# A selective-scan layer with a grouped expert layer: the scan's matmuls 64 rows wide, and LayerNorm and softplus work moved in two instruction queues

## The chip, the cores and the metric

The kernel runs on one core of one Trainium2 chip. A core has TensorE (PE in the profile, its weight loads PEld), VectorE (DVE), ScalarE (ACT), GpSimd (POOL) and SyncE (SP), which here issues the DMA transfers. Each engine works through its own list of instructions in order, and semaphores tie the lists together. The metric is the device time of one execution in microseconds.

## The reference

The input x is 16 sequences of 1024 tokens with 512 channels. It is normalised once (xn), and two branches are added to it. The second branch (routing tokens to experts) lies in the later phases of the kernel, which the change does not touch. The first is a chunked selective scan:

```python
def _forward(x, W_in, dt_W, dt_b, A_log, D_param, W_out, norm_w):
    proj = x @ W_in.T            # xp, z, B_ssm, C_ssm, dt_low
    dt = jax.nn.softplus(dt_low @ dt_W.T + dt_b)
    dA = dtc * A
    dAcs = jnp.cumsum(dA, axis=2)
    ...
    scores = jnp.einsum('bcihn,bcjhn->bcijh', Cc, Bc) * Lm * dtc[:, :, None, :, :]
    y_intra = jnp.einsum('bcijh,bcjhp->bcihp', scores, xc)
    ...
    y_cross = jnp.einsum('bcthn,bchnp,bcth->bcthp', Cc, h_states, jnp.exp(dAcs))
    y = (y_intra + y_cross).reshape(B, S, H, P)
    y = y + xp * D_param[None, None, :, None]
    y = y.reshape(B, S, D_INNER)
    rms = jnp.sqrt(jnp.mean(y * y, axis=-1, keepdims=True) + 1e-06)
    y = y / rms * norm_w
    y = y * jax.nn.silu(z)
    return y @ W_out.T
...
x = x + _L0_attn_ref(xn, ...) + _L0_ffn_ref(xn, ...)
```

There are 16 heads of 32 channels, 16 states per head, and chunks of 64 tokens.

## The kernel before

The kernel has three phases: the scan layer (to about 2170 us), the gather and the scatter of the expert layer (the rest). All three parts of the change lie in the first phase.

The first phase handles 128 tiles of 128 tokens (two chunks each), two tiles to a superstep, so 64 supersteps `s` and two more to drain. In superstep s every engine works on three generations at once: tiles 2s and 2s+1 (n0: projections, step sizes), tiles 2(s-1) and 2(s-1)+1 (n1: scores, states, scan), and tiles 2(s-2) and 2(s-2)+1 (n2: gate, output projection, residual). The order of the work is written out by hand for each engine, in a loop over s.

- TensorE, per superstep: `project_bdt`, `transpose_xn`, `transpose_b`, `project_x`, `transpose_yz`, `chunk_states`, `scores`, `project_z`, `project_out`, `sums`, `scan`, and then much the same for the second tile of each pair. `transpose_yz(n2)` writes the bank `mix` that `lo_xn` reads, so it waits for `lo_xn`. `scores` waits for `expand_c`. `sums(s)` waits for `dA_ready`, the last of POOL's `step_sizes`, and stands right ahead of `scan(n1)`. `scan(n)` waits for `mask_scores(n)`. Each fp32 matmul of `scan`, `scores` and `chunk_states` is recorded as two instructions.
- VectorE: `scale_y`, `lo_xn`, `expand_c`, `gate`, `stats`, `finish_stats`, `normalize`, `lo_yz`, `states`, `mask_scores`, `residual`, `states`, `scale_y`, and the same for the second tile; `picks(s)` ends the superstep. `stats(n)` waits for the DMA that brings tile n of x; `normalize` for POOL's `inv_std`; `lo_yz` for ScalarE's `hi_yz`.
- SyncE issues the load of x tile 2(s+2) only after it has issued the store of `residual(n2)`, and the load of tile 2(s+2)+1 only after `picks(s)` and the store of `residual(n2+1)`. The DVE reads tile 2(s+2) in superstep s, and tile 2(s+2)+1 in superstep s+1.
- ScalarE: after the bias is added by POOL (`add_bias`) it takes Abs, Relu and Exp of it, then `hi_yz(n2)`, `copy_x`, Ln and Exp (which need POOL's `exp_low`), `spread_c`.
- GpSimd: `add_skip`, `add_bias`, `inv_std`, `exp_low`, `spread_c`, `step_sizes`, `skip_x`, `inv_rms`, `scale_b`, `add_skip`, `inv_std`, `spread_c`, `skip_x`, `inv_rms`.

Of the kernel before, what the change touches and what calls it, by code (L numbers as in the profile page):

```python
# [32 lines left out]
H, HD, NS, R = 16, 32, 16, 16  # L33
DI = H * HD
KI = DI // P
CH = 64
# [55 lines left out]
def attention_phase(nc, io, keep, sems):  # L92
# [5 lines left out]
    with ExitStack() as ctx:  # L98
        scan_bank = ctx.enter_context(nc.psum_tensor("a_scan", [P, 4, 512], F32))
# [4 lines left out]
    HALF = 256  # L104
# [6 lines left out]
    scan_in = [sb(f"scan_in{c}", [P, H, CH]) for c in range(2)]  # L111
# [50 lines left out]
    xs = [[sb(f"xs{c}_{j}", [P, H, HD]) for j in range(4)] for c in range(2)]  # L162
# [109 lines left out]
    def valid(s):  # L272
        return 0 <= s < NST

    def token_rows(c):
        return slice(CH * c, CH * c + CH)
# [16 lines left out]
    def states_ready(n, c):  # L293

        return 4 + 8 * n + 4 * c
# [48 lines left out]
    def gpsimd_program(pool, gather):  # L344
# [23 lines left out]
        def skip_x(n):  # L368

            pool.wait_ge(x_cp, n + 1)  # L370
            wait(pool, yv_cp, n)
            for c in range(2):
                rows_ = token_rows(c)
                nc.gpsimd.tensor_tensor(dx[rows_, :], xs[c][n % 4][rows_, :, :].rearrange("t h d -> t (h d)"), d_row[rows_, :],  # L374
                                        ALU.mult).then_inc(dx_cp, 1)
                pool.wait_ge(dx_cp, 2 * n + c + 1)
# [65 lines left out]
        for s in range(NST + 2):  # L442
            n1, n2 = 2 * (s - 1), 2 * (s - 2)
            add_bias, exp_low, step_sizes = soft_plus(s)
            if valid(s - 2):
                add_skip(n2 + 1)
            if valid(s):
                add_bias()
            if valid(s + 1):
                inv_std(2 * (s + 1) + 1, 1)  # L450
            if valid(s):
                exp_low()
            if valid(s - 1):
                spread_c(n1)
            if valid(s):
                step_sizes()
            if valid(s - 1):
                skip_x(n1)
            if valid(s - 2):
                inv_rms(n2 + 1, 1)  # L460
            if valid(s):
                scale_b(s)
            if valid(s - 1):
                add_skip(n1)
            if valid(s + 2):
                inv_std(2 * (s + 2), 0)
            if valid(s - 1):
                spread_c(n1 + 1)
                skip_x(n1 + 1)
                inv_rms(n1, 0)  # L470
# [147 lines left out]
    def vector_program(dve):  # L618
# [14 lines left out]
        def stats(n):  # L633
            dve.wait_ge(x_in[n % (2 * STB)], 16 * (n // (2 * STB) + 1))
            wait(dve, xn_ready, n - 1)
            nc.vector.bn_stats(bst[:, n % 2, :], x_tile(n)).then_inc(ln, 1)
            dve.wait_ge(ln, 2 * n + 1)

        def finish_stats(n):
            nc.vector.bn_aggr(mv[:, n % 2, :], bst[:, n % 2, :]).then_inc(ln, 1)  # L640
# [8 lines left out]
        def lo_xn(n, b, i):  # L649
            dve.wait_ge(xnT_hi, n + 1)  # L650
            nc.vector.tensor_tensor(xnT[b][1][:, :, i * P:(i + 1) * P], mix[:].rearrange("p (k t) -> p k t", k=KD),
                                    xnT[b][0][:, :, i * P:(i + 1) * P].bitcast(F32), ALU.subtract).then_inc(xnT_lo, 1)
# [41 lines left out]
        def scale_y(n):  # L694

            dve.wait_ge(y_ps, 2 * n + 2)
            wait(dve, yv_cp, n)
            gain = e1[:, n // 2 % 2, n % 2, :].rearrange("p (b h) -> p b h", b=2).unsqueeze(3).to_broadcast([P, 2, H // 2, HD])
            nc.vector.tensor_tensor(yt[:].rearrange("p (b h d) -> p b h d", b=2, h=H // 2),  # L699
                                    scan_bank[:, 2:4, HALF:512].rearrange("p b (h d) -> p b h d", h=H // 2), gain,  # L700
                                    ALU.mult).then_inc(yt_cp, 1)
# [51 lines left out]
        for s in range(NST + 2):  # L753
            n0, n1, n2 = 2 * s, 2 * (s - 1), 2 * (s - 2)
            par = s % 2
            gains, next_gains = mg[:, 1 - par, :, :], mg[:, par, :, :]
            if valid(s - 2):
                scale_y(n2 + 1)
            if valid(s + 1):
                lo_xn(2 * (s + 1), 1 - par, 0)  # L760
            if valid(s - 1):
                expand_c(n1)
            if valid(s - 2):
                gate(n2 + 1)
            if valid(s + 1):
                stats(2 * (s + 1) + 1)
                finish_stats(2 * (s + 1) + 1)
                normalize(2 * (s + 1) + 1)
            if valid(s - 2):
                lo_yz(n2)  # L770
            if valid(s - 1):
                dve.wait_ge(mg_ready, s)
                states(n1, 0, gains[:, :, 1:2], gains[:, :, 2:3])
                mask_scores(n1)
            if valid(s - 2):
                residual(n2, 0)
            if valid(s - 1):
                states(n1, 1, gains[:, :, 3:4], gains[:, :, 4:5])

                scale_y(n1)  # L780
            if valid(s + 1):
                lo_xn(2 * (s + 1) + 1, 1 - par, 1)
            if valid(s - 1):
                expand_c(n1 + 1)
                gate(n1)
            if valid(s + 2):
                stats(2 * (s + 2))
                finish_stats(2 * (s + 2))
            if valid(s - 2):
                lo_yz(n2 + 1)  # L790
            if valid(s - 1):
                states(n1 + 1, 0, gains[:, :, 5:6], gains[:, :, 6:7])
                mask_scores(n1 + 1)
            if valid(s + 2):
                normalize(2 * (s + 2))
            if valid(s - 2):
                residual(n2 + 1, 1)
            if valid(s - 1):
                if valid(s):
                    dve.wait_ge(mg_ready, s + 1)  # L800
                    states(n1 + 1, 1, gains[:, :, 7:8], None if s % STB == 0 else next_gains[:, :, 0:1])
            if s == 0:
                stage_lo(LAST_STAGE)
            if valid(s):
                picks(s)

    def tensor_program(pe, gather):
# [113 lines left out]
        def scan(n):  # L921

            pe.wait_ge(mt_cp, 4 * n + 4)
            pe.wait_ge(cs_cp[0], n + 1)
            pe.wait_ge(cs_cp[1], 2 * n + 2)
            pe.wait_ge(g_ready, states_ready(n, 1))
            for h in range(H):
                for c in range(2):
                    for i in range(0, CH, 32):
                        out = scan_bank[CH * c + i:CH * c + i + 32, 2 + h // 8, HALF + h % 8 * HD:HALF + (h % 8 + 1) * HD]  # L930
                        last = nc.tensor.matmul(out, scan_in[c][:, h, i:i + 32], xs[c][n % 4][:, h, :], start=True, stop=True)  # L931
                    if h == H - 1:
                        last.then_inc(y_ps, 1)

# [662 lines left out]
```

## Time and profile before

| | |
|---|---|
| time, median of 3 runs | 3144.28 us (3142.84 to 3148.3) |
| the profiled execution's own time | 3142.84 us |
| its span | 3140.9 us |
| PE busy | 2957.3 us, 94% |
| PEld busy | 2523.2 us, 80% |
| DVE busy | 2407.3 us, 77% |
| ACT busy | 1587.4 us, 51% |
| POOL busy | 1283.6 us, 41% |
| share of PE in the chain that ended last | 82% |
| share of DVE in it | 10% |

The span runs from the first to the last instruction of the program. The chain that ended last is followed back from the last instruction to whatever released each step. The busy time of PE is modelled for pipelined matmuls, so how long a stretch of matmuls takes is read from the start of one group to the start of the next.

### The profile page before, as it was taken

What the parts mean: (1) busy time and instruction counts of PE and PEld (TensorE: products, weight loads), DVE (VectorE), ACT (ScalarE), POOL (GpSimd) and SP (SyncE); (2) the same over time, 40 slices, a digit from 0 to 9 for tenths busy, and PEclk for the clock granted to TensorE, in tenths of its full rate; (3) what the DMA queues carried; (4) which work ended last, traced back from release to release, by engine and by line L of the source; (5) the groups of instructions that cost most, each with busy time, mean ns of one, the idle gap of its engine ahead of it and who ended that gap; (6) DMA issues with size and microseconds to landing.
All of it is one profiled execution on the core that took longest, in us unless ns stands there. A gap on an engine that the chain in (4) does not pass through costs nothing.

```text
span 3140.9 us, 134679 instructions
## 1 busy us (share of the span) xinstructions
PE 2957.3 (94%) x59784; PEld 2523.2 (80%) x59784; DVE 2407.3 (77%) x3546; ACT 1587.4 (51%) x3614; POOL 1283.6 (41%) x2029
## 2 busy tenths in 40 slices
PE   7999999999999999999999999997878877999999
PEld 6888888888888888888888888885766666888887
DVE  5888888888888988898888888885444436777775
ACT  4555555555555555555555555553333322555555
POOL 3555565655555655556555555553000001000000
PEclk9999999999999999999999999998999997999999
DMA  3221111111111111111111111114444435768765
GB/s 113 71 61 48 55 51 51 55 48 55 54 44 55 54 47 55 51 50 53 51 55 51 48 57 52 47 43 173 134 118 119 109 110 154 228 211 236 223 206 156
DMA packets 336546, 286.94 MB, mean 91 GB/s; under 512 B 52304, under 2 KB 265808, under 8 KB 335072
## 3 DMA queue, kind: packets, MB, share of 16 engines
q1 hardware_dynamic: 335392, 278.16, 29.8%
q8 instruction: 473, 7.75, 1.0%
q14 instruction: 105, 0.86, 0.1%
q10 hardware_dynamic: 576, 0.17, 0.0%
HBM read 165.01 MB, written 113.25 MB: 89 GB/s over the span
## 4 chain that ended last, share of the span: by engine, by line
PE 82%; DVE 10%; issue 5%; DMA 1%; POOL 1%; SPq 0%; ACT 0%; DVEq 0%; POOLq 0%; ACTq 0%
PE a_proj L811 34%; PE a_mix L811 9%; PE s_rt L1462 8%; PE g_pick_ps L1223 5%; PE a_scan L931 5%; PE s_w_ps L1448 5%; PE s_sum L1475 4%; DVE g_picked L1192 3%; PE g_acc_ps L1244 2%; DVE scan_in L673 2%; PE a_scan L908 2%; DVE xs L691 2%; PE a_scan L895 2%; PE a_mix L819 2%; PE a_mix L883 2%
## 5 line engine op out<-in xcount | busy, mean ns | idle before, releaser
L691 DVE TENSOR_SCALAR xs<-gs,mg 64x128 f32<-64x128 f32 x960 | 546.7, 628 | 8.8
L811 PE MATMUL a_proj<-wdh,xnTh 128*128 128x512 f32 x1024 | 424.3, 414 | 1.4 <-DVE wdl L627 0.7
L1418 DVE TENSOR_TENSOR s_resT<-s_w_ps,s_b 128x2048 f32<-128x2048 f32 x128 | 293.4, 2292 | 154.3 <-PE s_w_ps L1448 154.3
L1412 ACT COPY s_res<-s_rt 128x512 f32<-128x512 f32 x512 | 263.0, 600 | 290.0 <-PE s_rt L1462 290.0
L811 PE MATMUL a_proj<-wdh,xnTl 128*128 128x512 f32 x1024 | 405.9, 396 | 0.7 <-issue 0.7
L811 PE MATMUL a_proj<-wdl,xnTh 128*128 128x512 f32 x1024 | 404.7, 395 | 0.6 <-issue 0.6
L673 DVE COPY_PREDICATED scan_in<-mask,a_scan 64x512 f32<-64x512 uint32 x512 | 377.5, 737 | 16.0
L382 POOL TENSOR_TENSOR yv<-yt,dx 128x512 f32<-128x512 f32 x128 | 166.6, 1302 | 418.3 <-DVE yt L699 418.3
L374 POOL TENSOR_TENSOR dx<-xs,d_row 64x512 f32<-64x512 f32 x256 | 329.3, 1286 | 15.1
L1192 DVE COPY g_picked<-g_pick_ps 128x1024 f32<-128x1024 f32 x128 | 156.7, 1224 | 224.9 <-PE g_pick_ps L1223 224.9
L540 ACT ACTIVATE scan_in<-CT,hsel 64x128 f32<-64x128 f32 x1024 | 325.9, 388 | 4.8
L365 POOL TENSOR_TENSOR scan_in<-CT,hsel 64x512 f32<-64x512 f32 x256 | 267.1, 1044 | 10.2
L505 ACT COPY raw<-a_proj 128x272 f32<-128x272 f32 x128 | 49.5, 387 | 419.3 <-PE a_proj L811 419.3
L1170 ACT COPY g_picked<-g_pick_ps 128x1024 f32<-128x1024 f32 x128 | 129.6, 1013 | 249.9 <-PE g_pick_ps L1223 249.3
L1462 PE MATMUL s_rt<-s_ident,s_resT 128*128 128x128 f32 x2048 | 255.2, 278 | 0.0
L1462 PEld LDWEIGHTS s_rt<-s_ident,s_resT 128*128 128x128 f32 x2048 | 219.7, 141 | 30.6 <-issue 25.4
L811 PEld LDWEIGHTS a_proj<-wdh,xnTh 128*128 128x128 f32 x1024 | 195.0, 190 | 46.6 <-issue 11.5
L811 PEld LDWEIGHTS a_proj<-wdh,xnTl 128*128 128x128 f32 x1024 | 194.8, 190 | 45.0 <-issue 1.3
L811 PEld LDWEIGHTS a_proj<-wdl,xnTh 128*128 128x128 f32 x1024 | 195.3, 191 | 34.5 <-issue 1.5
L811 PE MATMUL a_proj<-xnTh,wth 128*128 128x256 f32 x768 | 222.0, 289 | 0.0
L811 PE MATMUL a_mix<-woh,ygh 128*128 128x512 f32 x512 | 210.9, 412 | 8.9 <-DVE ygl L711 8.9
L811 PE MATMUL a_proj<-xnTh,wtl 128*128 128x256 f32 x768 | 215.8, 281 | 0.0
(121 smaller groups left out, 6839.3 us busy)
## 6 DMA issues: line engine op xcount, KB each, us to landing
x<-in_x_dram SPq DMA_DIRECT2D x128, 256.0 KB, 3.4
xn_dram<-xn SPq DMA_DIRECT2D x128, 256.0 KB, 2.4
part_dram<-res SPq DMA_DIRECT2D x128, 256.0 KB, 2.9
g_xn<-xn_dram SPq DMA_DIRECT2D x128, 256.0 KB, 3.0
s_w<-in_w_dram SPq DMA_DIRECT2D x128, 256.0 KB, 3.9
s_part<-part_dram SPq DMA_DIRECT2D x128, 256.0 KB, 3.7
out_dram<-s_out SPq DMA_DIRECT2D x128, 256.0 KB, 2.8
g_w<-in_w_dram SPq DMA_DIRECT2D x4, 2048.0 KB, 12.8
```

The lines of the kernel that those rows point to most:

```text
L365: nc.gpsimd.tensor_tensor(c_places(1, w), src, sel, ALU.mult).then_inc(cs_cp[1], 1)
L374: nc.gpsimd.tensor_tensor(dx[rows_, :], xs[c][n % 4][rows_, :, :].rearrange("t h d -> t (h d)"), d_row[rows_, :], ALU.mult).then_inc(dx_cp, 1)
L382: nc.gpsimd.tensor_tensor(yv[:], yt[:], dx[:], ALU.add).then_inc(yv_cp, 1)
L540: last = nc.scalar.activation(dst[:, :, j, :], CT[own, n % 4, :, 0:CH], ACT.Copy, scale=hsel4[own, j:j + 1])
L673: nc.vector.copy_predicated(dst, mask[rows_, :].unsqueeze(1).unsqueeze(1).to_broadcast([CH, 4, 2, CH]), src).then_inc(mt_cp, 1)
L691: nc.vector.tensor_scalar(dst, gs[rows_, q, :].unsqueeze(1).to_broadcast([CH, 2, 2 * HD]), scale0[rows_, q, :], scale1[rows_, q, :], ALU.m ...
L811: last = nc.tensor.matmul(out, lhs[a], rhs[c], start=(k == 0 and n == 0), stop=(k == nk - 1 and n == 2))
L931: last = nc.tensor.matmul(out, scan_in[c][:, h, i:i + 32], xs[c][n % 4][:, h, :], start=True, stop=True)
L1192: nc.vector.tensor_copy(picked_view(n, tq, 1), pick_view(1)).then_inc(pick_cp[1], 1)
L1412: nc.scalar.copy(res[:, n % 4, :, :], rt_bank[n % 3][:].rearrange("p (n d) -> p n d", n=GPT)).then_inc(res_cp, 1)
L1418: nc.vector.tensor_tensor(resT[m % 2][:, :, sets].rearrange("p n (q r) -> p n q r", r=4), w2_bank[:].rearrange("p r q n -> p n q r"), b2[: ...
L1462: last = nc.tensor.transpose(rt_bank[n % 3][:, g * P:(g + 1) * P], resT[m % 2][:, place_of(GPT * t + g), :], ident[:])
```

## The change

It has three parts. On TensorE, `scan(n)` computes each head and chunk in one matmul with 64 output rows, where it took two with 32 rows each. On VectorE, `stats` of either tile of a pair moves ahead of `lo_xn`, `expand_c` and `gate`, with `lo_xn` between `stats` and `finish_stats`; `normalize` of the odd tile stays behind `gate`. On GpSimd, `add_bias` moves behind `inv_std`, `spread_c` ahead of `exp_low`, and `skip_x` ahead of `step_sizes`.

```diff
@@ gpsimd_program @@
             if valid(s - 2):
                 add_skip(n2 + 1)
-            if valid(s):
-                add_bias()
             if valid(s + 1):
                 inv_std(2 * (s + 1) + 1, 1)
             if valid(s):
+                add_bias()
+            if valid(s - 1):
+                spread_c(n1)
+            if valid(s):
                 exp_low()
             if valid(s - 1):
-                spread_c(n1)
+                skip_x(n1)
             if valid(s):
                 step_sizes()
-            if valid(s - 1):
-                skip_x(n1)
@@ vector_program @@
             if valid(s + 1):
+                stats(2 * (s + 1) + 1)
                 lo_xn(2 * (s + 1), 1 - par, 0)
+                finish_stats(2 * (s + 1) + 1)
             if valid(s - 1):
                 expand_c(n1)
             if valid(s - 2):
                 gate(n2 + 1)
             if valid(s + 1):
-                stats(2 * (s + 1) + 1)
-                finish_stats(2 * (s + 1) + 1)
                 normalize(2 * (s + 1) + 1)
...
+            if valid(s + 2):
+                stats(2 * (s + 2))
             if valid(s + 1):
                 lo_xn(2 * (s + 1) + 1, 1 - par, 1)
+            if valid(s + 2):
+                finish_stats(2 * (s + 2))
             if valid(s - 1):
                 expand_c(n1 + 1)
                 gate(n1)
-            if valid(s + 2):
-                stats(2 * (s + 2))
-                finish_stats(2 * (s + 2))
@@ tensor_program, scan(n) @@
             for h in range(H):
                 for c in range(2):
-                    for i in range(0, CH, 32):
-                        out = scan_bank[CH * c + i:CH * c + i + 32, 2 + h // 8, HALF + h % 8 * HD:HALF + (h % 8 + 1) * HD]
-                        last = nc.tensor.matmul(out, scan_in[c][:, h, i:i + 32], xs[c][n % 4][:, h, :], start=True, stop=True)
+                    last = nc.tensor.matmul(scan_bank[token_rows(c), 2 + h // 8, HALF + h % 8 * HD:HALF + (h % 8 + 1) * HD],
+                                            scan_in[c][:, h, :], xs[c][n % 4][:, h, :], start=True, stop=True)
```

## Rows read from the trace of the kernel before

**Rows 1.** Stretch: us, busy of PE, PEld, DVE, ACT, POOL, clock, DMA share, GB/s.

```profile
62.00:2170.00 2108.00, 2062.68 (x36780) 1752.37 (x36766) 1826.32 (x3090) 1147.84 (x2893) 1203.05 (x1942) 0.99 0.18 52
```

**Rows 2.** One line, L939 (`sums`, eight instructions a superstep): durations, first and last start.

```profile
L939 PE MATMUL a_misc<-dA,umat x512: 196/206/217, 34.9 to 2121.0; 128*32 128x32 f32 x171
```

**Rows 3.** Who waited for whom: us in total, times, longest us.

```profile
DVE xn L646 <- POOL mv L355: 62.7, 67, 1.1
DVE bst L636 <- DMA x<-in_x_dram: 52.7, 59, 3.1
...
PE a_misc L949 <- issue: 19.4, 13, 2.1
...
PE a_scan L931 <- DVE scan_in L673: 16.9, 19, 2.0
```

**Rows 4.** Timeline of PE in one superstep: start us, us, instruction group, idle before it.

```profile
1059.59 1.30 PE L931 MATMUL a_scan<-xs,scan_in 128*32 128x32 f32 x128
1060.81 0.66 PE L819 MATMUL a_mix<-a_ident,xn 128*128 128x128 f32 x4
1061.40 0.44 PE L949 MATMUL a_misc<-logs,hexp 128*32 128x8 f32 x32
1061.77 0.50 PE L811 MATMUL a_proj<-wdh,xnTh 128*128 128x512 f32 x1
```

**Rows 5.** Groups of weight loads by shape: busy us, mean ns of one.

```profile
L811 PEld LDWEIGHTS a_proj<-wdh,xnTh 128*128 128x128 f32 x1024 | 195.0, 190 | 46.6 <-issue 11.5 <-DVE wdl L627 0.9
L931 PEld LDWEIGHTS a_scan<-xs,scan_in 128*32 128x32 f32 x16384 | 153.7, 109 | 32.3 <-DVE scan_in L673 20.2 <-issue 2.7
...
L908 PEld LDWEIGHTS a_scan<-cexp,BT 32*64 32x64 f32 x4096 | 58.1, 131 | 11.8 <-issue 0.2
```

**Rows 6.** Timeline of DVE over one superstep, from picks to picks.

```profile
1046.43 0.42 DVE L732 TENSOR_TENSOR permT<-lg,gmax 128x256 bf16<-128x256 f32 x1
...
1047.85 0.69 DVE L651 TENSOR_TENSOR xnTl<-a_mix,xnTh 128x512 fp32r<-128x512 f32 x1 [0.40 <-ACT xnTh L475]
...
1050.85 0.70 DVE L636 BATCH_NORM_STATS2 bst<-x 128x6 f32<-128x512 f32 x1 [0.85 <-DMA x<-in_x_dram]
...
1052.69 0.55 DVE L646 TENSOR_SCALAR xn<-x,mv 128x512 f32<-128x512 f32 x1 [0.93 <-POOL mv L355]
...
1053.87 0.43 DVE L683 TENSOR_TENSOR gs<-a_scan,xs 64x256 f32<-64x256 f32 x1
1054.33 2.12 DVE L691 TENSOR_SCALAR xs<-gs,mg 64x128 f32<-64x128 f32 x4
...
1059.56 0.75 DVE L718 SCALAR_TENSOR_TENSOR res<-a_mix,rms,x 128x512 f32<-128x512 f32 x1
...
1063.11 0.68 DVE L651 TENSOR_TENSOR xnTl<-a_mix,xnTh 128x512 fp32r<-128x512 f32 x1
...
1067.85 4.53 DVE L691 TENSOR_SCALAR xs<-gs,mg 64x128 f32<-64x128 f32 x4
...
1076.06 0.75 DVE L718 SCALAR_TENSOR_TENSOR res<-a_mix,rms,x 128x512 f32<-128x512 f32 x1
...
1079.29 0.42 DVE L732 TENSOR_TENSOR permT<-lg,gmax 128x256 bf16<-128x256 f32 x1
```

**Rows 7.** The x loads (L342): the timeline's issue, and all 124 from issue to landing.

```profile
1047.74 0.51 SPq L342 DMA_DIRECT2D x<-in_x_dram  x1
```

```profile
DMA to landing us min/median/max: 2.7/3.4/4.7
```

**Rows 8.** Timeline of POOL, and one row of ACT, in the same superstep.

```profile
1049.20 0.88 POOL L397 TENSOR_TENSOR v<-raw,dtb_row 128x16 f32<-128x16 f32 x2 [0.37 <-ACT raw L505]
...
1053.62 2.15 POOL L365 TENSOR_TENSOR scan_in<-CT,hsel 64x512 f32<-64x512 f32 x2
...
1057.08 2.65 POOL L374 TENSOR_TENSOR dx<-xs,d_row 64x512 f32<-64x512 f32 x2
```

```profile
1052.15 0.59 ACT L551 CAST ygh<-a_mix 128x512 fp32r<-128x512 f32 x1 [0.95 <-PE a_mix L883]
```

More of the change, by code:

```diff
@@ L451, in gpsimd_program @@
             if valid(s):
-                exp_low()
+                add_bias()
             if valid(s - 1):
@@ L455, in gpsimd_program @@
             if valid(s):
-                step_sizes()
+                exp_low()
             if valid(s - 1):
                 skip_x(n1)
+            if valid(s):
+                step_sizes()
             if valid(s - 2):
```

## The prediction

> **What bounds the kernel now.** I first read the busy times by stretch. In the first phase, 62 to 2170 us, TensorE is busy 2063 of 2108 us at a granted clock of 0.99, DVE 1826, ACT 1148, POOL 1203 [rows 1]. TensorE sets the pace there. DVE is second: over 64 supersteps it has (2108 − 1826) / 64 = 4.4 us of idle time each. The length of a superstep comes from one line that runs once in each: from 34.9 to 2121.0 us in 63 steps, 33.11 us [rows 2]. The waits say how thin the margin is: TensorE stands still little (16.9 us for the masked scores, 19.4 us in the small matmuls of `spread_gains` with no releaser, "issue") [rows 3]. The DVE waits more, but TensorE does not feel it: 52.7 us in 59 places for the load of x, 62.7 us for POOL's `inv_std` [rows 3]. Each of 59 supersteps therefore has a moment when the x tile arrives later than DVE wants it. That is the most important row for this change. Last I followed one undisturbed superstep through the timelines of DVE, POOL, ACT, SyncE and TensorE [rows 4, 6, 7, 8].
>
> I call E the end of `picks`, 1046.43 + 0.42 = 1046.85, and M the start of the first residual, 1059.56, so M = E + 12.7. The next E is 1079.71, M + 20.15, and this superstep has 32.86 us [rows 6].
>
> **The scan on TensorE.** It removes 64 of 128 recorded instructions per scan, two scans a superstep. Now a scan takes 1060.81 − 1059.59 = 1.22 us [rows 4], and in it the four groups of 32 array columns take turns, 32 rounds of 4 instructions. What limits a round? The neighbour L949 has the same weight shape, 128*32, with only 8 moving columns where the scan has 32. Its 32 instructions take 1061.77 − 1061.40 = 0.37 us, a quarter of the scan's number in 0.30 of its time [rows 4]. Moving columns are not the limit, so it is the load of weights or the issue of instructions. The loads last 109 ns with 32 columns, 131 with 64, 190 with 128 [rows 5]: (190 − 109) / 96 = 0.84 ns a column, or (131 − 109) / 32 = 0.69. If each half of the array can take one load at a time, the 32 rounds (now of 2 instructions) each get longer by 32 columns: 32 × 32 × 0.84 = 0.86 us, or by the flatter slope 0.70. If instructions are the limit, the scan halves: −0.61 us. The loads are long in comparison, and equal for both neighbours, so I take the first, +0.8 us a scan; the bounds are −0.6 and +0.86. With TensorE as the bound and nothing else changed that is 128 × 0.8 = +102 us.
>
> **`stats` moved ahead, first tile of the superstep (n = 2(s+1)+1).** The work is the same, but DVE is a queue. The load for this `stats` is issued only after `picks`: at 1047.74, E + 0.9 [rows 7], and `stats` starts on its landing at 1050.85, E + 4.0 [rows 6]. This time is tied to E whatever DVE does in between. Today `lo_xn`, `expand_c` and `gate` lie in that gap and only 0.40 + 0.85 us of it is idle [rows 6]. After the change only `scale_y` (0.6 us) is left there; DVE stands still for 3.4 us, and behind it stand `lo_xn`, for which TensorE's `transpose_yz` waits, and `expand_c`, for which `scores` waits. What is given back: the three waits of 0.40, 0.85 and 0.93 us ahead of `lo_xn`, `stats` and `normalize` [rows 6]. DVE's work from E to the first `gs` is 1053.87 − 1046.85 − 2.18 = 4.84 us; with `scale_y` in the gap, `gs` would start at E + 4.0 + 4.24 = E + 8.2, against E + 7.0 today.
>
> **The moved POOL work adds a second delay.** `finish_stats` ends about E + 4.0 + 0.7 + 0.7 + 0.1 = E + 5.5 (`stats` 0.70, `lo_xn` 0.69 [rows 6]). `inv_std` takes 0.9 of it (DVE's wait 0.93 [rows 6]), to E + 6.4. Only then comes `add_bias`, 0.88 [rows 8], to E + 7.3. ScalarE's three small operations need it (about 0.5 us; my estimate, well below one 0.59 operation each), and behind them in ScalarE's queue stands `hi_yz`, 0.59 [rows 8]: E + 8.45. `lo_yz` waits for that and takes 0.7, so `gs` starts at E + 9.2, not 8.2. Today `add_bias` starts at 1049.20, ahead of `inv_std`, and none of this is waited for.
>
> On POOL `spread_c` (2.15), `exp_low` (about 1.0), `skip_x` (2.65) and `step_sizes` (the 1.31 us between `spread_c`'s end and `skip_x`'s start today) follow [rows 8]: E + 7.3 + 2.15 + 1.0 + 2.65 + 1.3 = E + 14.4 for `dA_ready`. `sums` waits for it, and right behind `sums` waits the scan. Today it is there at 1057.1, E + 10.3 [rows 8]. This alone would let the scan start at E + 14.8.
>
> **`states` meets other POOL work.** Its four operations take 2.12 us in one place and 4.53 us in another [rows 6]; in the second POOL runs `spread_c` and `skip_x` beside it all the way. Today `skip_x` starts at 1057.08, after the first `states` [rows 8]. After the change it starts at E + 10.5 while `states` runs from E + 9.7. From (4.53 − 2.12) / 3 = 0.8 us for each further POOL operation met, I add one, 0.8; bounds 0 and 2.4. The Trainium skill ("SBUF — State Buffer", Who interferes with whom) says that DVE in a two-port mode and GpSimd exclude each other for a whole instruction, and that issue order decides who blocks. The two durations above agree with that; what it adds is that POOL may be the one held up, and the sum by rule and row is the same in size.
>
> From `gs` to M is 1059.56 − 1053.87 = 5.69 us today [rows 6]. So the new M is E + 9.2 + 5.69 + 0.8 = E + 15.7, against E + 12.7. The scan (from E + 14.8 at the earliest) follows the mask at about M.
>
> **The second `stats` (n = 2(s+2)).** Its load is issued behind the store of the first residual: M + 0.75 + 0.4, and lands 3.4 us later, median [rows 7], so about M + 4.6. DVE reaches `stats` after `scale_y`, at 1063.11 − 1059.56 = M + 3.55 [rows 6]: a new wait of 1.1 us. Behind it, `states` is at its expensive 4.53 us; POOL gets `inv_std` earlier relative to it, so it should meet one POOL operation less, −0.8. TensorE starts its scan with M and is 0.8 us later after it; the second residual starts at M + 16.5 [rows 6] and may be delayed by that. I take M to the next E unchanged, 20.15 us; bounds −0.3 and +1.1.
>
> **The sum.** New superstep: 15.7 + 20.15 = 35.85 us. TensorE alone would need about 33.11 − (16.9 + 19.4) / 63 + 1.6 = 34.1, so the loop through DVE binds and the dearer scan is mostly covered by it; if that cover were gone it would cost its 1.6 us a superstep. (35.85 − 33.11) × 63 = +173 us. The profiled execution took 3142.84 us (span 3140.9), so 3142.84 + 173 = 3316, say 3315 us; the median of the runs shown is 1.4 us above the profiled one. Later phases don't change. By the bounds: M at E + 14.9 (`states` meets nothing) and 19.85 behind it give 34.75, +103; E + 17.3 and 20.65 give 37.95, +305. For this case alone I hold 3245 to 3410.
>
> **The rivals.**
>
> *Only the scan counts.* The DVE's wait is swallowed after all, as if TensorE could run further behind DVE, and only the wider scan is left. For it: DVE has 4.4 us of idle time a superstep, and I spend 2.7 beyond it. Against it: the wait is tied to `picks` through SyncE, so it can't be shifted. +102 us less the stalls that a slower TensorE gives back (16.9 + 19.4): 3142.8 + 66 = 3209, up to 3245.
>
> *Faster.* Instructions, not weight loads, limit the scan, and the arrival of x is early enough. 128 × −0.61 = −78 us and part of the 36 us of stalls, 3142.8 − 78 − 20 = 3045. The place is the scan, and it decides if the span from one scan to the next group falls under 1.22 us and the x load lands within 0.6 us of `picks`; rows 7 put it at 4.0. The Trainium skill ("TensorEngine Tiling (Array Packing)", Instruction Overhead) has a rule in its favour: about 60 cycles of overhead for each small matmul, whatever its free size. By that rule the number of instructions in each column group would be all that counts, the weights' width nothing; the scan would then stay at 1.22 us, since each half of the array still gets 32 instructions.
>
> *Nothing measurable.* The scan is level by that reckoning (32 rounds as now) and DVE's wait hidden: 3143.
>
> **How the numbers follow.** The DVE loop 0.74 (3245 to 3410); only the scan 0.15 (3195 to 3245); nothing 0.03; faster 0.08. What a measurement can tell from no change is 0.2%, 6 us. The range 3200 to 3400 leaves out the last two and the top end of the first. Faster 0.08, same 0.03, slower 0.89.
>
> **What would show it.** In the changed profile: `sums` recurring every 35.8 us or so; the wait of DVE's `stats` for the x load at about 64 × 3.4 + 64 × 1.1 = 290 us in place of 52.7; the waits of `normalize` for POOL near 0; new waits of TensorE for `lo_xn` or `expand_c`, for `dA`, and for the mask; a scan of about 2.0 us with 64 instructions. What would make it wrong: a superstep near 34 us with `stats` waiting for little (then the loop is not tied as I say), a scan at 1.2 us or below (then loads are not its limit), or `states` and POOL blocking each other far more than in one place.

## The result, and the profile after

The changed kernel takes 3273.86 us (median of 4 runs, 3265.9 to 3279.61) against 3143.56 us for the kernel before on the same chip. The ratio is 1.041, with a 95% interval of 1.0385 to 1.0442: it is 4.1% slower. The profiled execution took 3265.26 us. Of the four executions of one kernel below, e12, one took 6023.18 us and is left out of its ratio, though not of its median; why it took so long is not known.

The head of the page of the changed kernel, then its first phase as a stretch (columns as in [rows 1]) and the row of `sums`:

```profile
span 3263.5 us, 118480 instructions
...
PE 3052.7 (94%) x51592; PEld 2615.3 (80%) x51592; DVE 2255.0 (69%) x3546; ACT 1578.3 (48%) x3614; POOL 1347.6 (41%) x2029
```

```profile
62.00:2200.00 2138.00, 2076.11 (x27458) 1775.08 (x27457) 1607.35 (x2978) 1100.47 (x2796) 1220.43 (x1884) 1.00 0.17 49
```

```profile
L939 PE MATMUL a_misc<-dA,umat x512: 195/216/263, 36.8 to 2244.3; 128*32 128x32 f32 x171
```

`sums` now recurs every (2244.3 − 36.8) / 63 = 35.04 us, against 33.11 [rows 2]. That is +1.93 × 63 = +122 us, which is the whole difference of the two profiled executions (3265.26 − 3142.84 = 122.4). DVE, the engine that was to become the bound, is busy less: 1607 of 2138 us. Its groups show part of why. The row of `states` in the table of the costliest groups says 546.7 us, 628 ns each, before, and after:

```profile
L691 DVE TENSOR_SCALAR xs<-gs,mg 64x128 f32<-64x128 f32 x960 | 444.4, 525 | 8.8
```

The waits of the changed kernel (us in total, times, longest), to be held against [rows 3]:

```profile
DVE bst L636 <- DMA x<-in_x_dram: 283.0, 124, 4.9
...
PE a_misc L939 <- POOL dA L417: 60.2, 63, 4.5
...
DVE xn L646 <- POOL mv L355: 32.6, 67, 1.1
```

`stats` waits for the x load 283 us, as forecast. TensorE has a new wait of 60 us, for `dA`. Its wait for DVE's mask, 16.9 us before, and its "issue" stalls before L949, 19.4 us before [rows 3], are all but gone: its waits have no row for L949 any more, and the whole list of its idle time before the bank `a_scan` is this.

```profile
  DVE scan_in L673: 2.3, 2
  DVE cexp L659: 1.6, 1
  issue: 0.6, 2
```

DVE in one superstep that begins at E = 1070.38 + 0.42 = 1070.80 (columns as in [rows 6]; these rows answer to those):

```profile
1070.38 0.42 DVE L732 TENSOR_TENSOR permT<-lg,gmax 128x256 bf16<-128x256 f32 x1
...
1075.29 0.69 DVE L636 BATCH_NORM_STATS2 bst<-x 128x6 f32<-128x512 f32 x1 [3.89 <-DMA x<-in_x_dram]
1076.02 0.69 DVE L651 TENSOR_TENSOR xnTl<-a_mix,xnTh 128x512 fp32r<-128x512 f32 x1
...
1078.42 0.61 DVE L646 TENSOR_SCALAR xn<-x,mv 128x512 f32<-128x512 f32 x1 [0.44 <-POOL mv L355]
1079.78 0.69 DVE L711 TENSOR_TENSOR ygl<-a_mix,ygh 128x512 fp32r<-128x512 f32 x1 [0.75 <-ACT ygh L551]
1080.51 0.43 DVE L683 TENSOR_TENSOR gs<-a_scan,xs 64x256 f32<-64x256 f32 x1
1080.97 1.18 DVE L691 TENSOR_SCALAR xs<-gs,mg 64x128 f32<-64x128 f32 x4
1082.18 3.03 DVE L673 COPY_PREDICATED scan_in<-mask,a_scan 64x512 f32<-64x512 uint32 x4
1085.24 0.75 DVE L718 SCALAR_TENSOR_TENSOR res<-a_mix,rms,x 128x512 f32<-128x512 f32 x1
```

`stats` starts at E + 4.5 after 3.9 us of waiting, `gs` at E + 9.7, and M, the start of the first residual, is E + 14.4. Between them lies what the forecast had not expected: `states` takes 1.18 us, not the 2.12 of before or the 2.9 of the forecast.

The chain that ended last, over the first half of the same superstep (start, us, what):

```profile
1070.38 0.43 DVE permT L732
1070.83 0.33 SPq L336
...
1071.20 0.43 SPq L339
...
1071.68 3.59 DMA x<-in_x_dram
1075.29 0.70 DVE bst L636
...
1076.88 0.55 POOL ve L353
...
1077.51 0.88 POOL mv L355
1078.39 0.36 POOL v L397 x2
1078.75 1.17 POOL scan_in L365
...
1082.07 1.25 POOL dx L374
...
1085.63 0.41 POOL dA L417 x2
...
1086.53 2.06 PE a_scan L930 x64
```

This is the loop that sets the superstep: `picks`, SyncE's stores, the x load, `stats`, `inv_std`, `add_bias`, `spread_c`, `exp_low`, `skip_x`, `step_sizes`, then `sums` and the scan on TensorE, and from there TensorE to the next `picks`. DVE's mask, done just before 1085.24, is not in it. A scan, from its start to the next group's, now takes 1088.52 − 1086.53 = 1.99 us:

```profile
1086.53 2.06 PE L930 MATMUL a_scan<-xs,scan_in 128*64 128x32 f32 x64
1088.52 0.66 PE L820 MATMUL a_mix<-a_ident,xn 128*128 128x128 f32 x4
```

The averages below are over 53 supersteps of each trace, worked out from the times of the instructions. P is the superstep, the columns up to M are us after E: the starts of `stats`, `gs`, the scan and the residual, all the first of the superstep, and the end of dA. "Second half" is P less the start of the first scan.

| kernel | P | `stats` | `gs` | dA | scan | M | second half |
|---|---|---|---|---|---|---|---|
| before | 33.23 | 4.07 | 7.26 | 10.35 | 13.01 | 12.98 | 20.22 |
| after | 35.14 | 4.15 | 9.36 | 14.88 | 15.22 | 14.29 | 19.92 |

### The profile page after: what moved, and what is told of

It is laid out like the page before. It is cut to its first block, busy times and chain, and to the rows that moved or that the text cites. A ratio compares the mean times of both kernels' runs of the same rounds, so it can differ in the third digit from the quotient of the medians.

```text
span 3263.5 us, 118480 instructions
## 1 busy us (share of the span) xinstructions
PE 3052.7 (94%) x51592; PEld 2615.3 (80%) x51592; DVE 2255.0 (69%) x3546; ACT 1578.3 (48%) x3614; POOL 1347.6 (41%) x2029
## 3 DMA queue, kind: packets, MB, share of 16 engines
q1 hardware_dynamic: 335392, 278.16, 28.5%
## 4 chain that ended last, share of the span: by engine, by line
PE 53%; POOL 16%; DVE 13%; issue 8%; DMA 6%; SPq 2%; ACT 1%; DVEq 0%; POOLq 0%; ACTq 0%
PE a_proj L812 15%; PE s_rt L1462 7%; DMA x<-in_x_dram 6%; PE g_pick_ps L1223 5%; POOL dx L374 5%; PE a_mix L812 5%; PE s_w_ps L1448 4%; POOL scan_in L365 4%; PE a_scan L930 4%; PE s_sum L1475 4%; DVE g_picked L1192 3%; DVE xs L691 3%; PE g_acc_ps L1244 2%; POOL mv L355 2%; DVE bst L636 1%
## 5 line engine op out<-in xcount | busy, mean ns | idle before, releaser
L691 DVE TENSOR_SCALAR xs<-gs,mg 64x128 f32<-64x128 f32 x960 | 444.4, 525 | 8.8
L374 POOL TENSOR_TENSOR dx<-xs,d_row 64x512 f32<-64x512 f32 x256 | 329.7, 1288 | 15.2
L636 DVE BATCH_NORM_STATS2 bst<-x 128x6 f32<-128x512 f32 x128 | 88.8, 694 | 287.0 <-DMA x<-in_x_dram 283.0
L365 POOL TENSOR_TENSOR scan_in<-CT,hsel 64x512 f32<-64x512 f32 x256 | 277.6, 1084 | 10.0
L930 PE MATMUL a_scan<-xs,scan_in 128*64 128x32 f32 x8192 | 265.1, 224 | 2.6 <-DVE scan_in L673 2.3
L930 PEld LDWEIGHTS a_scan<-xs,scan_in 128*64 128x64 f32 x8192 | 251.8, 139 | 14.6 <-DVE scan_in L673 4.1
L812 PEld LDWEIGHTS a_proj<-wdh,xnTh 128*128 128x128 f32 x1024 | 193.2, 189 | 45.2 <-issue 10.8
```

The costliest lines, as they stand in the source:

```text
L365: nc.gpsimd.tensor_tensor(c_places(1, w), src, sel, ALU.mult).then_inc(cs_cp[1], 1)
L691: nc.vector.tensor_scalar(dst, gs[rows_, q, :].unsqueeze(1).to_broadcast([CH, 2, 2 * HD]), scale0[rows_, q, :], scale1[rows_, q, :], ALU.m ...
L812: last = nc.tensor.matmul(out, lhs[a], rhs[c], start=(k == 0 and n == 0), stop=(k == nk - 1 and n == 2))
L930: last = nc.tensor.matmul(scan_bank[token_rows(c), 2 + h // 8, HALF + h % 8 * HD:HALF + (h % 8 + 1) * HD], scan_in[c][:, h, :], xs[c][n % ...
```

## The experiments

The diff has three parts: the wide scan, the two moved `stats` on DVE, and POOL's order. The first three kernels are before with one part alone.

**The scan alone (e1).**

```diff
-                    for i in range(0, CH, 32):
-                        ... scan_in[c][:, h, i:i + 32] ...
+                    ... scan_in[c][:, h, :] ...
```

> The kernel before with the wide scan alone. Loop theory (DVE and POOL orders make the long loop, TensorE is the bound without them): TensorE's own list becomes the superstep, 33.11 + 2 x 0.77 us less the stalls it gives back (36 us over the phase), about 34.1 us, so +60 us, 3200 us, up to +98 us. Additive rival (each part costs its own share of +122 us): anything, but the sum of the three single parts must be about +122 us. If issue of instructions were the limit: faster by up to 78 us.

Measured: ratio 1.0164 [1.0144, 1.0184], 3192.94 us. In its row

```profile
L938 PE MATMUL a_misc<-dA,umat x512: 196/206/217, 35.4 to 2171.1; 128*32 128x32 f32 x171
```

a superstep has 33.90 us (table's mean 34.00), close to the 34.1 that the prediction gave TensorE by itself.

**DVE's order alone (e2).**

```diff
             if valid(s + 1):
+                stats(2 * (s + 1) + 1)
                 lo_xn(2 * (s + 1), 1 - par, 0)
+                finish_stats(2 * (s + 1) + 1)
...
+            if valid(s + 2):
+                stats(2 * (s + 2))
...
```

> The kernel before with the DVE order alone. Loop theory: VectorE stands still for the x load (stats waits about 280 us in all), gs starts about 1.3 us later after picks, dA is early again; the loop is then about 33.2 to 34.3 us, +10 to +75 us, middle 3180 us. Rival (the wait for x is what costs, whatever POOL does): nearly all of the +122 us, about 3245 to 3265 us.

Measured: 1.0339 [1.0315, 1.0364], 3247.39 us, superstep 35.08.

```profile
DVE bst L636 <- DMA x<-in_x_dram: 304.6, 124, 4.9
...
PE a_mix L884 <- issue: 66.6, 55, 2.3
```

The time is that of the rival (3245 to 3265), not the 3180 expected. The second row is TensorE waiting in `transpose_yz`. The profile names no releaser, but the times do:

```profile
1083.19 0.69 DVE L651 TENSOR_TENSOR xnTl<-a_mix,xnTh 128x512 fp32r<-128x512 f32 x1
...
1083.98 0.30 PE L884 MATMUL a_mix<-a_ident,yz 128*128 128x128 f32 x1 [1.85 <-issue]
```

`transpose_yz` starts 0.10 us after `lo_xn` ends, here and in 54 of the 55 places. It writes the bank that `lo_xn` reads, and the second `stats` now keeps `lo_xn` waiting. The wait is 54.5 us in e12 and 27.0 in e7, but only 5.9 in the changed kernel.

**POOL's order alone (e3).**

```diff
-                add_bias()
...
                 inv_std(2 * (s + 1) + 1, 1)
...
+                add_bias()
...
+                spread_c(n1)
...
                 exp_low()
...
-                spread_c(n1)
+                skip_x(n1)
...
                 step_sizes()
...
-                skip_x(n1)
```

> The kernel before with the POOL order alone. Loop theory: dA comes behind x load, inv_std, add_bias, spread_c, exp_low and skip_x, about 13.9 us after picks instead of 10.3, TensorE waits for it a little: superstep about 33.5 us, 3168 us (3145 to 3190). Rival (POOL has 40% idle time, so its order is free): 3143 us.

Measured: 1.0231 [1.0206, 1.0256], 3212.46 us, superstep 34.18.

```profile
PE a_misc L939 <- POOL dA L417: 36.5, 44, 3.8
```

Its dA comes at E + 13.4, 3.1 us later than before, though no `stats` was moved. The time lies above the 3145 to 3190 expected. Part of it may be the clock: its profiled execution has the lowest mean granted clock of all kernels here, 0.973 (before 0.983). Each part alone makes the kernel slower: 1.6, 3.4 and 2.3%, which is 7.3% as a sum, against 4.1% for all three. So the parts are not independent, and the next kernels ask which pair shares its cost.

**All but the scan (e4)**, after with the narrow scan put back:

```diff
-                    ... scan_in[c][:, h, :] ...
+                    for i in range(0, CH, 32):
+                        ... scan_in[c][:, h, i:i + 32] ...
```

> The changed kernel with the old scan of 32-row matmuls (DVE and POOL orders alone). Loop theory: the loop x load, stats, POOL's chain to dA, TensorE's scan to its second output projection, residual, picks holds one scan, so it gets shorter by one scan's 0.77 us a superstep: 35.04 - 0.77 = 34.3 us, about 49 us less than the changed kernel, 3217 us. Rival of the prediction (the loop runs through DVE's mask, the dearer scan is covered): no change against 3265 us. Additive rival: the single parts gave +49, +103 and +68 us; DVE and POOL together would be +171, 3315 us.

Measured: 1.0536 [1.0515, 1.0556], 3303.72 us. Putting the cheaper scan back made the kernel slower than the changed one. The expectation had the wrong sign; the additive rival, 3315, is the nearest. Its rows:

```profile
PE a_misc L940 <- POOL dA L417: 91.2, 62, 4.4
...
PE a_misc L950 <- issue: 28.5, 13, 2.6
```

```profile
62.00:2200.00 2138.00, 1979.23 (x34633) 1669.63 (x34635) 1541.70 (x2923) 1082.40 (x2745) 1197.46 (x1850) 0.98 0.16 49
```

TensorE waits 91 us for dA and is stalled 28.5 us before L950 and, by the list of idle time before `a_scan`, 24.4 us before the scan, with no releaser. The granted clock fell to 0.98 where after has 1.00. One of the places, in the timeline of PE:

```profile
1041.89 0.31 PE L950 MATMUL a_misc<-logs,hexp 128*32 128x8 f32 x15 [1.90 <-issue]
...
1042.93 0.40 PE L812 MATMUL a_proj<-wdh,xnTh 128*128 128x512 f32 x1
...
1043.85 0.63 PE L812 MATMUL a_proj<-wdh,xnTh 128*128 128x512 f32 x1
1044.28 0.63 PE L812 MATMUL a_proj<-wdl,xnTh 128*128 128x512 f32 x1
```

After an idle time of 1.9 us the same matmuls go from 0.23 to 0.43 us apart: the clock went from 2.4 to 1.2 GHz for 3.4 us. There are 17 such spells in this trace from 62 to 2200 us, each behind an idle time of TensorE of 0.9 to 4.3 us. The trace of after has one, near its start; from 100 us on its longest idle time is 1.5 us.

What the stalls without a releaser wait for can be read from the trace's DMA records. In the stretch from 1039.4 to 1040.6 us, around the start of the stall shown, there is one transfer of the queue that brings instructions (transfers, MB, share of the DMA engines):

```profile
q8 instruction: 1, 0.02, 4.6%
```

It ends at 1040.46, and TensorE goes on 1.43 us later. All 30 such stalls of over 0.5 us in e4 (62 to 2200 us, `transpose_yz` left out) end 1.2 to 1.6 us after the end of such a transfer; so do 19 of 19 in e11 and 21 of 22 in before. That interval covers 6% of the time, and of the 59 waits of over 0.5 us in e4 that have a named releaser none ends in it. The queue is TensorE's: after has 8192 fewer matmuls than e4 and as many fewer weight loads, and this queue 64 transfers fewer (409 against 473), so one transfer holds 256 instructions. These stalls are TensorE waiting for its own instructions.

**Scan and POOL (e5), scan and DVE (e6).**

Each is the edit of e1 on top of e3's or of e2's:

```diff
-                        ... scan_in[c][:, h, i:i + 32] ...
+                    ... scan_in[c][:, h, :] ...
...
-                add_bias()
...
                 inv_std(2 * (s + 1) + 1, 1)
...
+                add_bias()
...
```

> The changed kernel with the old DVE order. Loop theory: POOL order alone gave +68 us, so the loop through dA is there without the DVE's new place for stats; it holds one scan, so +68 + 49 us, 3260 us. Rival (TensorE's list is the bound in both single kernels): the larger of the two, 3212 us.

> The changed kernel with the old POOL order. If the loop through DVE's mask binds with the DVE order alone (+103 us), the dearer scan is covered but for what TensorE takes behind the mask: 3247 to 3275 us. Additive rival: +103 + 49, 3296 us.

Measured: e5 1.0201 [1.0184, 1.0218], 3201.0 us; e6 1.0291 [1.0274, 1.0308], 3229.11 us. Both lie below what was expected (3260, and 3247 to 3275). The wide scan costs 1.6% alone. Added to DVE's order it gives back 0.5% (e6 against e2, 1.0339), and added to both 1.2%. Added to POOL's order it costs nothing that can be measured (e5 against e3, 1.0231 [1.0206, 1.0256]: the intervals overlap).

**Is the scan limited by weight loads? (e9).** Before, with the scan's loop over i outermost: 128 instructions as before, but only two column groups take turns instead of four.

```diff
-            for h in range(H):
-                for c in range(2):
-                    for i in range(0, CH, 32):
+            for i in range(0, CH, 32):
+                for h in range(H):
+                    for c in range(2):
```

> The kernel before, its scan in the order i outermost: the same 128 instructions with 32 columns each, but only two of the four 32-column groups take turns at a time. If the round is limited by the load of the weights' columns (34.6 ns a round of 32 columns, as before), a scan takes 64 rounds, about 2.2 + 0.1 us, and the time rises by about 128 x 1.1 us less stalls, 3245 us. If a group's round has a fixed length whatever the columns when two groups take turns (58 ns, as in the changed kernel), a scan takes 3.8 us and the time is near 3440 us. If issue of instructions limits, no change: 1.22 us and 3143 us.

Measured: 1.0208 [1.0185, 1.0232], 3206.91 us; superstep 34.25. In the timeline of PE a scan, from its first instruction at 1089.69, takes 2.08 us to the next group (mean 2.06), 64 rounds of about 32 ns (a round is one recorded matmul on each column group in turn); before has 1.22 [rows 4].

```profile
1089.73 2.10 PE L931 MATMUL a_scan<-xs,scan_in 128*32 128x32 f32 x127
1091.77 0.66 PE L819 MATMUL a_mix<-a_ident,xn 128*128 128x128 f32 x4
```

The time stayed under the 3245 expected: a scan grew by 0.84 us and not by 1.1, and the stalls before L949 fell from 19.4 to 7.7 us. The same instructions as before, in another order, cost 0.8 us more a scan. So neither the count of instructions nor their issue sets the 1.22 us; a column group takes a new weight of 32 columns every 32 to 38 ns (2.06 us / 64 rounds here, 1.22 / 32 before [rows 4]), and one of 64 columns every 62 ns (1.99 / 32 in after).

**The x load earlier (e7 on after, e8 on before).** The load of the second tile no longer stands behind the store that waits for `picks`:

```diff
             for i in range(2):
-                if i == 1 and valid(s):
-                    sync.wait_ge(pm, 3 * s + 3)
-                    sync.dma_start(perm_dram[s], permT ...)
...
                 if valid(s + 2): ... x load ...
+                if i == 1 and valid(s):
+                    sync.wait_ge(pm, 3 * s + 3)
+                    sync.dma_start(perm_dram[s], permT ...)
```

> The changed kernel; SyncE issues the second tile's x load ahead of the store of picks, so it is tied to the second residual (2.9 us before the end of picks) and not to picks. Loop theory: x lands about 1 us after picks instead of 3.9, the wait of stats for it falls from 283 us to about 100 us, the loop gets up to 2.8 us shorter and TensorE's own list binds: 3193 us as with the wide scan alone, up to 3205 us. Rival (the load is covered, POOL's own order costs the time): 3265 us.

Measured: 1.0444 [1.0429, 1.046], 3276.48 us. The gain expected (3193 to 3205) did not come, though the load's wait halved and dA's all but vanished (5.8 us); another wait took their place:

```profile
DVE bst L636 <- DMA x<-in_x_dram: 140.6, 94, 3.5
...
PE a_scan L930 <- DVE scan_in L673: 52.7, 63, 2.0
```

The first `stats` now starts at E + 1.1 and dA comes at E + 12.7, 2.2 us earlier, but M is at E + 15.0, later than in after. The first `states` takes 3.16 us, where it takes 1.18 in after.

> The kernel before; SyncE issues the second tile's x load ahead of the store of picks. TensorE's list binds already; what can go are its stalls for the mask (16.9 us) and some of the clock losses that follow them: 3115 to 3135 us against 3136 to 3144. Rival (DVE's waits of 52.7 us count in full): about 3090 us. Rival (nothing is on the path): no change.

Measured: 0.9948 [0.9929, 0.9967], 3126.51 us, as expected.

```profile
L939 PE MATMUL a_misc<-dA,umat x512: 190/196/218, 35.0 to 2104.5; 128*32 128x32 f32 x171
```

That is 32.85 us a superstep. The wait for the mask fell from 16.9 to 5.2 us, that for the load from 52.7 to 5.6. This version beats both kernels, before by 0.5% and after by 4.5% (0.9948 / 1.0413 = 0.955).

**Both load waits out of after (e10)**, e7 with the second `stats` put back:

```diff
+            if valid(s + 1):
+                lo_xn(2 * (s + 1) + 1, 1 - par, 1)
+            if valid(s - 1):
+                expand_c(n1 + 1)
+                gate(n1)
             if valid(s + 2):
                 stats(2 * (s + 2))
-            if valid(s + 1):
-                lo_xn(2 * (s + 1) + 1, 1 - par, 1)
-            if valid(s + 2):
                 finish_stats(2 * (s + 2))
-            if valid(s - 1):
-                expand_c(n1 + 1)
-                gate(n1)
```

> The changed kernel with the earlier x load for the second tile (as in the run that moved the wait but not the time) and with the second stats back in its old place behind gate. Theory: in that run the loop went over to the other load, tied to the first residual (stats waited 140.6 us in all, the first states met POOL for 3.16 us instead of 1.18). Without that wait both loops are open and TensorE's list binds as with the wide scan alone: 34.0 to 34.3 us a superstep, 3193 to 3212 us. Rival (POOL's meeting with states, not the load, is what keeps it up): 3250 us or more.

Measured: 1.0371 [1.0348, 1.0394], 3256.55 us. The 3193 to 3212 expected was missed, and the rival (3250 or more, from the meeting of POOL and `states`) holds. Load waits are down to 21.8 us, and still TensorE waits:

```profile
PE a_scan L929 <- DVE scan_in L673: 58.9, 64, 3.6
```

The timelines of DVE and of POOL show the meeting that the prediction had put into the changed kernel:

```profile
1075.13 3.30 DVE L691 TENSOR_SCALAR xs<-gs,mg 64x128 f32<-64x128 f32 x4
```

```profile
1072.04 2.15 POOL L365 TENSOR_TENSOR scan_in<-CT,hsel 64x512 f32<-64x512 f32 x2
...
1075.12 2.64 POOL L374 TENSOR_TENSOR dx<-xs,d_row 64x512 f32<-64x512 f32 x2
```

`states` and `skip_x` start together and `states` takes 3.30 us: its first two operations take 1.35 and 1.44 us and end 0.08 us after the two pieces of `skip_x`, the other two take 0.41 and 0.35. The Trainium skill ("SBUF — State Buffer", Who interferes with whom) says that VectorE in a two-port mode and GpSimd exclude each other on a shared port for whole instructions. The durations here, 3.30 with company and 1.18 without, agree; which mode VectorE ran in, no trace here shows.

**Which of two reasons makes after faster than e4? (e11)** e4 with e9's order in the scan: the pace of the wide scan with the number of instructions of the narrow one.

```diff
-            for h in range(H):
-                for c in range(2):
-                    for i in range(0, CH, 32):
+            for i in range(0, CH, 32):
+                for h in range(H):
+                    for c in range(2):
```

> DVE and POOL orders as changed, and a scan of the same 128 recorded instructions as before but spread over 2.05 us (two column groups at a time) instead of 1.23. The changed kernel was faster than the same with the old scan, 1.0413 against 1.0536. Theory A: the old scan takes 256 instructions in 1.1 us and outruns the delivery of TensorE's instructions, 23 + 28.5 us of stalls without a releaser, and the clock falls behind them; it is the pace that counts, so this kernel comes out near the changed one, 1.040 to 1.046. Theory B: the number of instructions counts: near 1.053 or above it, since the scans are slower as well.

Measured: 1.0535 [1.0511, 1.0559], 3311.17 us, level with e4 and not with after, so the pace is not the whole reason. But this kernel's clock is 1.00 in the first phase, and its stalls are half of e4's (10.4 us before the scan and 14.7 before L950), so the pace does something; the next section has the sum.

```profile
PE a_misc L950 <- issue: 14.7, 13, 1.6
```

**The second moved `stats` alone (e12)**, on before:

```diff
+            if valid(s + 2):
+                stats(2 * (s + 2))
             if valid(s + 1):
                 lo_xn(2 * (s + 1) + 1, 1 - par, 1)
+            if valid(s + 2):
+                finish_stats(2 * (s + 2))
             if valid(s - 1):
                 expand_c(n1 + 1)
                 gate(n1)
-            if valid(s + 2):
-                stats(2 * (s + 2))
-                finish_stats(2 * (s + 2))
```

> The kernel before with the second hunk of the DVE order alone (stats of the first tile ahead of lo_xn, expand_c and gate). With the whole DVE order the stretch from the first residual to the third gs grew by 0.67 us, that from picks to the first residual by 1.16 us. Theory: the two hunks share the cost about 1 : 2, so 3170 to 3185 us. Rival (only the load tied to picks costs): 3143 us.

Measured: 1.0181 [1.0158, 1.0204], 3201.3 us, more than the 3170 to 3185 expected, and over half of what DVE's order costs in e2.

```profile
PE a_mix L884 <- issue: 54.5, 40, 2.2
```

The averages, worked out as in the first table:

| kernel | P | `stats` | `gs` | dA | scan | M | second half |
|---|---|---|---|---|---|---|---|
| e1 scan | 34.00 | 4.33 | 8.08 | 10.62 | 13.98 | 13.83 | 20.02 |
| e2 DVE | 35.08 | 4.14 | 8.45 | 11.72 | 14.16 | 14.14 | 20.92 |
| e3 POOL | 34.18 | 3.99 | 7.91 | 13.44 | 13.77 | 13.13 | 20.41 |
| e4 DVE, POOL | 35.80 | 4.17 | 9.38 | 14.90 | 15.23 | 14.14 | 20.57 |
| e7 after, load | 35.40 | 1.08 | 8.32 | 12.69 | 15.07 | 15.04 | 20.33 |
| e10 | 34.99 | 0.94 | 8.30 | 12.69 | 15.12 | 15.10 | 19.87 |
| e11 | 36.02 | 4.29 | 9.54 | 15.05 | 15.40 | 14.52 | 20.62 |
| e12 | 34.20 | 4.20 | 7.68 | 10.50 | 13.46 | 13.42 | 20.74 |
| e8 before, load | 32.99 | 3.30 | 7.08 | 9.57 | 12.87 | 12.83 | 20.12 |

## Why the prediction was right, and where its sum was not

**Right: the scan's time.** 1.99 us against 2.0, and the width of the weights sets it: (1.99 − 1.22) / 32 rounds / 32 columns is 0.75 ns a column, between the prediction's two slopes of 0.69 and 0.84. e9 shows that the number of instructions does not. One premise fails, "If each half of the array can take one load at a time": before and e9 give each half the same 64 loads of 32 columns and take 1.22 and 2.06 us. It is the column group of 32, not the half, that takes one at a time, and in before four of them load side by side.

The rival that had the scan stay at 1.22 us, because each column group gets as many instructions as before, falls. The Trainium skill ("TensorEngine Tiling (Array Packing)", Instruction Overhead) has some 60 cycles of overhead for each matmul, the same for 1 and for 60 moving columns. e9 and the changed kernel both speak against that as the price here: the width of the weights and the number of column groups in turn decide, and the measurement goes before the page. The prediction put this rule under "faster", though by its own working it left the scan as it was.

**Right: the wait of `stats`.** The load is tied to `picks`: `stats` at E + 4.15 in after, E + 4.07 in before, and the wait 283 us where 290 was forecast. The split was right too: 215 us at the first `stats` and 62 at the second in 63 supersteps, 3.4 and 1.0 us each (forecast 3.4 and 1.1). `gs` came at E + 9.36 (forecast 9.2) and dA at E + 14.88 (forecast 14.4).

**Wrong: "`states` meets other POOL work".** The step from `gs` to M was put at 5.69 + 0.8 = 6.49 us and measured 14.29 − 9.36 = 4.93; it was 5.72 before. The change shortens it by 0.8 us where I lengthened it by 0.8. The base was wrong first: the 2.12 us of before were themselves a price in company, with `spread_c` running from 1053.62 beside `states` from 1054.33 [rows 6, 8]. By the prediction's own times `spread_c` would be over at E + 9.45 and `states` would start at E + 9.7, so that meeting was to go. In the trace `states` runs from 1080.97 to 1082.15, `spread_c` ends at 1081.05 (the chain's two pieces of L365) and `skip_x` starts at 1082.07 (L374): `states` falls into the gap between them and has POOL's large operations beside it for 0.2 us in all. The meeting I added did not happen either: `states` by itself takes so little that it is nearly over when `skip_x` starts (E + 10.8 on average, forecast 10.5). e10 shows the price of a meeting, about 1 us for each operation of `states` that meets a piece of `skip_x`.

**Wrong by its size: "I take M to the next E unchanged, 20.15 us".** From M to the next E the mean was 20.25 before and is 20.85 after, +0.60. It is not the second `stats`: DVE's wait of 1.0 us is there, but TensorE stands still before `transpose_yz` for 5.9 us in all, 0.1 a superstep (e12, where that wait does count, has 54.5). It is the start of the scan. The forecast had it "at about M", as before (0.03 us behind), and in after it is 0.93 us behind M, because it waits for dA; from the scan to the next E the superstep is 0.30 us shorter. Together, M + 1.31 and the rest + 0.60 make the 1.91 us measured in these means, against 3.0 + 0 in the forecast.

**Wrong: "so the loop through DVE binds".** In after the mask is waited for twice in all, 2.3 us, and dA 63 times, 60.2 us; the scan starts at E + 15.22, 0.34 us behind dA and 0.9 behind M. The prediction had this loop too (a start "from E + 14.8 at the earliest") and took it for the second. It is the first, because the mask came earlier than I had it. The two are close: e7 shortens the loop through dA by 2.2 us and the mask's closes at E + 15.07, 0.15 us away, with nothing gained. Which of them binds was a difference of two estimates, each uncertain by more than that difference.

**Wrong in part: "the dearer scan is mostly covered by it".** TensorE's time from the start of one group to the start of the next, where the kernels differ (means over 60 supersteps, us):

| kernel | first scan | `spread_gains` | `project_x` | second scan | `project_out` and the wait for dA |
|---|---|---|---|---|---|
| before | 1.31 | 0.70 | 3.01 | 1.23 | 2.96 |
| after | 1.99 | 0.37 | 3.01 | 1.99 | 3.88 |
| e4 | 1.70 | 0.87 | 3.43 | 1.23 | 4.39 |
| e11 | 2.29 | 0.63 | 3.12 | 2.06 | 3.99 |

The second scan is covered: e4 saves 0.76 us on it and waits 0.51 longer for dA, so that the scan starts at E + 15.23 there and at 15.22 in after. The first scan lies in the chain and is not covered, but it is more than paid back: from its start to the end of `project_x` (with the transposes between, 0.6 us) e4 takes 6.64 us and after 5.96. With no stall and a full clock the narrow scan would take 5.2 there (an estimate: after's row with a scan of 1.23). So e4 loses 1.4 us a superstep in this stretch to its waits for instructions and to the clock that falls behind them, and after loses nothing.

e11 takes 6.63 us, as much as e4, of which its slower scan is 0.83. So the slower pace alone gives back 0.8 of the 1.4 us, which is what it costs; the other 0.6 goes only with the smaller number of instructions. The instruction queue has 473 transfers in before and e4 and 409 in after, and these stalls are in every kernel with the narrow scan and in none with the wide one.

**The range and the rivals.** The result, 3273.86, lies inside the range (3200 to 3400) and inside the forecast's own (3245 to 3410), 41 us under the point. That is in part luck: the loop that was priced does not bind, and of its two terms one was 1.4 us too long (M) and the other 0.7 too short (M to the next E). The upper bound was not what its parts give either: with the +1.1 us it states behind M it is 17.3 + 21.25 = 38.55 us, where 37.95 was written, and the 3410 held lies below both. The rival "only the scan counts" (3209) describes e1, at 3193, and not the changed kernel.

**What the change cost where.** The scan's part is measured at 1.6% alone but is not a cost in company. DVE's and POOL's orders together cost 5.4% (e4), close to the 5.7 of their sum: the wait for a load issued after `picks` is passed on by DVE to `gs` (+2.1 us) and by POOL to dA (+4.5 us), and the second half adds 0.35 us in e4, from the stalls and the clock. The second `stats` adds 0.5 us to the second half by itself (e12). In the changed kernel TensorE comes to `transpose_yz` later and waits there 0.1 us a superstep; no run takes the second `stats` alone out of it.

## What to carry to other kernels

When a load is issued only after the last instruction of a loop's round, its consumer has a fixed place in the round, and moving the consumer forward in an engine's queue only moves everything behind it back; look at the issue of the load first (e8: 0.5% by reordering two transfers, where moving both `stats` forward cost 3.4%). When two loops are within a microsecond of one another, price both and expect that opening one closes on the other (e7). And parts of a change that touch one cyclic schedule are measured together as well as apart: here a part that costs 1.6% alone gives back 1.2% beside the others. A stall that has no releaser can be held against the instruction queue's transfers before it is put down to anything else.

## What the runs showed of the hardware that was not expected

Small fp32 matmuls whose weights are 32 columns wide run at 1.22 us per 128 when four column groups take turns and at 2.06 us when two do (before, e9). TensorE stalls 13 times before the narrow matmuls of `spread_gains` in each kernel with the narrow scan, 1.5 us a time in before, 2.2 in e4 and 0.6 in e9, and not at all once the scan has half as many matmuls. These stalls end 1.2 to 1.6 us after a transfer of the instruction queue has ended. In e4 the granted clock fell to 1.2 GHz 17 times behind idle times of TensorE, where before had seven such spells (62 to 2130 us). The x load lands in 3.4 us (median) before and 3.0 after; in the traces of before, e4 and after, the loads that overlap a transfer of instructions take 3.7 to 4.2 us and the others 2.9 to 3.0 (medians). That is a correlation only.
